# Graph network with two expert layers: what the accumulating stores of the last expert layer wait for

## The reference

```python
rh = jax.nn.relu(features @ router_w1 + router_b1)
expert_logits = jax.nn.softmax(rh @ router_w2 + router_b2, axis=-1)
top_w, top_i = jax.lax.top_k(expert_logits, TOP_K)               # TOP_K = 2
routing_weights = jax.nn.softmax(top_w, axis=-1)
h1 = jax.nn.relu(jnp.einsum('bsd,edh->bseh', features, expert_w1) + expert_b1)
h2 = jax.nn.relu(jnp.einsum('bseh,ehf->bsef', h1, expert_w2) + expert_b2)
expert_out = jnp.einsum('bsef,efo->bseo', h2, expert_w3) + expert_b3
sel = jnp.take_along_axis(expert_out, top_i[:, :, :, None], axis=2)
combined = jnp.sum(sel * routing_weights[..., None], axis=2)
...
x = x + _L1_ffn_ref(_layernorm(x, axis=-1)[None], ...)[0]
```

## Time and profile before

| | before |
|---|---|
| median of 3 runs | 6241.84 us (6240.61 to 6241.86) |
| the profiled execution | 6241.7 us |
| its span | 6240.0 us |
| first matmul group `c` of the expert loop | 5856.15 us |
| first accumulating store, tile 0 | 5860.63 us |
| first store of tile 9 | 5922.40 us |
| first store of tile 53, the last | 6229.75 us |
| PE busy, 5860 to 5940 | 80.00 of 80.00 us |
| DMA to landing, accumulating stores | 2.7 / 3.9 / 5.6 us (min, median, max) |

### The profile page before, as it was taken

The page is one execution under the profiler, slowest core; times in us unless marked ns, Lnnn a source line. Parts: engine busy times, 40 slices in busy tenths (PEclk is TensorE's granted clock), DMA queues, the critical chain, the costliest instruction groups (busy, mean ns, idle before and its releaser), DMA issues.

```text
span 6240.0 us, 87374 instructions
## 1 busy us (share of the span) xinstructions
PE 5227.2 (84%) x24825; PEld 4399.8 (71%) x24825; DVE 3345.8 (54%) x9909; ACT 1339.5 (21%) x3057; POOL 3935.4 (63%) x4345
## 2 busy tenths in 40 slices
PE   0265767489999999989999899899999999987786
PEld 0154555267777777777888788678887888876675
DVE  9867566445555555455445543564454644537422
ACT  0011111011111111124223322241112411112343
POOL 5777777765555555588888885406765067745444
PEclk9977888699999999999999999999999999999898
DMA  1022122233333333711001100213333134365443
GB/s 43 24 78 81 56 60 58 84 105 98 98 100 99 98 99 100 77 43 46 17 17 31 46 17 19 84 49 102 105 99 98 49 102 117 110 96 144 101 76 53
DMA packets 323172, 465.00 MB, mean 75 GB/s; under 512 B 98998, under 2 KB 253050, under 8 KB 322866
## 3 DMA queue, kind: packets, MB, share of 16 engines
q0 software_dynamic: 163312, 261.71, 18.5%
q1 hardware_dynamic: 159554, 199.67, 10.6%
HBM read 359.22 MB, written 102.61 MB: 74 GB/s over the span
## 4 chain that ended last, share of the span: by engine, by line
PE 65%; DMA 12%; POOL 8%; DVE 8%; issue 4%; ACT 1%; DVEq 0%; SPq 0%; POOLq 0%; ACTq 0%
PE bank L2342 19%; PE bank L2353 14%; DMA scratch_sorted<-sb_FREE 7%; POOL scratch_sorted L1020 6%; PE bank L2388 6%; PE bank L2403 6%; PE bank L2570 6%; PE bank L2552 5%; PE bank L2695 3%; PE bank L2333 2%; DMA sb_rows<-scratch_xn,sb_row_of 2%; DMA out<-sb_work_KT,sb_srec 1%; DMA out<-sb_work_TM,sb_srec 1%; DVE sb_STATE L1495 1%; POOL out L1090 1%
## 5 line engine op out<-in xcount | busy, mean ns | idle before, releaser
L1027 POOL DMA_INDIRECT sb_rows<-scratch_xn,sb_row_of x1760 | 1717.7, 976 | 1435.2 <-PE bank L2388 605.8
L1020 POOL DMA_INDIRECT scratch_sorted<-sb_FREE x1564 | 1608.1, 1028 | 486.0 <-issue 334.9
L2353 PE MATMUL bank<-sb_work_FT,sb_W 128*128 128x250 f32 x4400 | 1010.6, 381 | 20.1 <-ACT sb_work_FT L1099 15.5
L1099 ACT ACTIVATE sb_HT<-bank,sb_cols 128x250 f32<-128x250 f32 x1333 | 553.7, 467 | 1987.3 <-PE bank L2552 1061.8
L2353 PEld LDWEIGHTS bank<-sb_work_FT,sb_W 128*128 128x128 f32 x4400 | 847.7, 194 | 135.9 <-ACT sb_work_FT L1099 23.2
L2342 PE MATMUL bank<-sb_W,sb_HT 128*125 128x256 f32 x4000 | 890.8, 379 | 0.7 <-ACT sb_HT L1099 0.7
L2342 PEld LDWEIGHTS bank<-sb_W,sb_HT 128*125 128x125 f32 x4000 | 750.4, 188 | 114.1 <-ACT sb_HT L1099 1.1
L2403 PE MATMUL bank<-sb_rows,sb_work_TM 128*125 128x257 f32 x1760 | 473.3, 393 | 70.5 <-DMA sb_rows<-scratch_xn,sb_row_of 67.7
L1764 DVE TENSOR_TENSOR sb_FREE<-sb_FREE,bank 125x257 f32 x440 | 186.1, 423 | 623.6 <-PE bank L2388 588.4
L1819 DVE TENSOR_TENSOR sb_STATE<-sb_STATE,bank 125x257 f32 x440 | 185.7, 422 | 620.8 <-PE bank L2403 590.1
L2388 PE MATMUL bank<-sb_rows,sb_work_TM 128*125 128x257 f32 x1760 | 441.1, 390 | 38.4 <-DMA sb_rows<-scratch_xn,sb_row_of 29.1
(11 more groups left out here) (382 smaller groups left out, 7034.2 us busy)
## 6 DMA issues: line engine op xcount, KB each, us to landing
sb_rows<-scratch_xn,sb_row_of POOLq DMA_INDIRECT x1760, 2.8
scratch_sorted<-sb_FREE POOLq DMA_INDIRECT x1564, 2.3
scratch_qT<-sb_work_QF SPq DMA_DIRECT2D x100, 250.0 KB
sb_work_QF<-scratch_qT SPq DMA_DIRECT2D x100, 250.0 KB
sb_HT<-scratch_zs SPq DMA_DIRECT2D x54, 261.0 KB, 3.1
sb_work_XC<-in_x SPq DMA_DIRECT2D x50, 250.0 KB
sb_work_ZT<-scratch_xn SPq DMA_DIRECT2D x50, 250.0 KB
sb_W<-in_L_mix_W SPq DMA_DIRECT2D x9, 1024.0 KB
```

The lines of the kernel that those rows point to most:

```text
L1020: nc.gpsimd.indirect_dma_start(out=sorted_d[e], out_offset=bass.IndirectOffsetOnAxis(ap=pos[e][0:n, c:c + 1], axis=0), in_=rec[e][0:n, 2 * ...
L1027: nc.gpsimd.indirect_dma_start(out=rows[:, t % RING, 0:D], out_offset=None, in_=table, in_offset=bass.IndirectOffsetOnAxis(ap=row_of[:, t: ...
L1099: return nc.scalar.activation(dst, source, func, **k)
L2353: ins = nc.tensor.matmul(dst[:, b, :], w[:, k0 + k, 128 * (b0 + b):128 * (b0 + b) + 128], source[:, k, :], start=(n == 0), stop=(n == 2 * ...
```

## The change

POOL's wait ahead of a tile's stores is for other tiles than before. A real tile waits for all tiles of the experts ahead of its own; a padding tile for all tiles ahead of it. How many these are is known only on the chip, so DVE makes a table of counts and POOL reads it.

- The one semaphore `result_added` becomes four, one for each slot of the ring of four; a slot's semaphore goes up by 32 with each of its tiles. DVE's waits for tiles t - 4 and t - 8 and SP's last wait name the slot's semaphore.
- The routing steps get one more, `began_at`, a copy of START.
- `results_due` on DVE, between the preparation of tile 0 and that of tile 1, makes the table `due_of` in ten dependent steps: for a padding tile `began_at` becomes the tile's own number, and then, for each slot q, the number of tiles ahead of `began_at` that used slot q, at least 1, times 32, as integers.
- On POOL, tiles 0 to 3 wait as before. From tile 4 on, four value loads read the tile's counts, after the waits for `at` and `y`, and four waits against these registers, each with a `hold`, stand in place of the one wait against a constant.

The diff, without the new names of tensors and semaphores:

```diff
@@ on SP, at the end @@
-            sp.wait_ge(result_added, 32 * NX)
+            for t in range(NX - XRING, NX):
+                wait(sp, added(t))
@@ names @@
-        result_added = sem("result_added")
+        result_added = [sem(f"result_added_{q}") for q in range(XRING)]
+
+        def added(t):
+            return result_added[t % XRING], 32 * (t // XRING + 1)
@@ on POOL @@
+            pool.wait_ge(order_step, XRING + 6)
             for t in range(NX):
                 q = t % XRING
                 wait(pool, x_dve.done("at", t))
                 wait(pool, x_act.done("y", t))
-                if t:
-                    pool.wait_ge(result_added, 32 * t)
-                hold(pool)
+                if t < XRING:
+                    if t:
+                        wait(pool, added(t - 1))
+                    hold(pool)
+                else:
+                    before = [pool.value_load(due_of[0:1, slot, t:t + 1], min_val=32, max_val=32 * (NX // XRING + 1))
+                              for slot in range(XRING)]
+                    for slot in range(XRING):
+                        pool.wait_ge(result_added[slot], before[slot])
+                        hold(pool)
                 for u in range(2):
                     nc.gpsimd.indirect_dma_start(
...
-                        compute_op=ALU.add).then_inc(result_added, 16)
+                        compute_op=ALU.add).then_inc(result_added[q], 16)
@@ on DVE @@
+            step("began_at", nc.vector.tensor_copy(began_at, START))
             step("exp_all", nc.vector.tensor_copy(exp_all, EXPERTS))
...
+            def results_due():
+
+                def due_step(n, ins):
+                    ins.then_inc(order_step, 1)
+                    dve.wait_ge(order_step, n)
+
+                late = due[:, 0, :]
+                due_step(1, nc.vector.tensor_tensor(late, turn_no, began_at, ALU.subtract))
+                due_step(2, nc.vector.scalar_tensor_tensor(late, real, 0.5, late, ALU.is_lt, ALU.mult))
+                due_step(3, nc.vector.tensor_tensor(began_at, began_at, late, ALU.add))
+                for q in range(XRING):
+                    due_step(4 + q, nc.vector.tensor_scalar(
+                        due[:, q, :], began_at, 1.0 / XRING, (XRING - 1 - q) / XRING - (XRING - 1) / (2.0 * XRING),
+                        ALU.mult, ALU.add))
+                due_step(XRING + 4, nc.vector.tensor_scalar(due, due, ROUND, ROUND, ALU.add, ALU.subtract))
+                due_step(XRING + 5, nc.vector.tensor_scalar(due, due, 1.0, 32.0, ALU.max, ALU.mult))
+                due_step(XRING + 6, nc.vector.tensor_copy(due_of, due))
...
             for b in range(-2, NX + 1):
                 t = b + 2
+                if t == 1:
+                    results_due()
...
-                        dve.wait_ge(result_added, 32 * (t - SRING + 1))
+                        wait(dve, added(t - SRING))
...
-                        dve.wait_ge(result_added, 32 * (t - XRING + 1))
+                        wait(dve, added(t - XRING))
```

More of the change, by code:

```diff
@@ L511, in build @@
         exp_all = carve(NX)
+        began_at = carve(NX, 1)
+        due = carve(XRING * NX, 1).rearrange("p (q t) -> p q t", q=XRING)
+        due_of = carve(XRING * NX, 1).bitcast(I32).rearrange("p (q t) -> p q t", q=XRING)
         SHARES = carve(4 * SRING).rearrange("p (q u k) -> p q u k", q=SRING, u=2)
@@ L575, in build @@
         tile_loaded = [sem(f"tile_loaded_{q}") for q in range(XRING)]
-        result_added = sem("result_added")
+        result_added = [sem(f"result_added_{q}") for q in range(XRING)]
+        def added(t):
+            return result_added[t % XRING], 32 * (t // XRING + 1)
         pads_stored, pads_ready = sem("pads_stored"), sem("pads_ready")
         route_step, route_sums = sem("route_step"), sem("route_sums")
-        out_stored, routing_cleared = sem("out_stored"), sem("routing_cleared")
+        out_stored, routing_cleared, order_step = sem("out_stored"), sem("routing_cleared"), sem("order_step")
         ROUTE_STEPS = ["tiles", "whole", "began", "ended", "done", "row", "real", "in", "rel", "in0",
-                       "last", "exp_of", "in_of", "exp_all"]
+                       "last", "exp_of", "in_of", "began_at", "exp_all"]
         def route(step):
```

## The result

| | before | after |
|---|---|---|
| median of 4 runs | 6241.85 us (6240.61 to 6242.10) | 6177.66 us (6176.16 to 6178.67) |
| ratio | | 0.9898, 95% interval 0.9886 to 0.9911 |
| the profiled execution, its span | 6241.7, 6240.0 us | 6176.16, 6174.4 us |
| first store of tile 0 | 5860.63 us | 5861.12 us |
| first store of tile 50 | 6210.81 us | 6144.74 us |

The kernel is 64 us faster, 1.0%. Forecast were 6176 us, in a range of 6168 to 6205.

What follows compares the result with a forecast made beforehand. POOL's wait for landing, 6.99 us a tile, bounds the later expert phase. Tile 50's store at 6144.4, plus 18.94, 0.5 and 10.25, gives a span of 6174.1; with 1.7 around it, 6176 us, range 6168 to 6205.

Steps and rivals of the forecast that it cites:

- The bound before: Expert phase, later part: POOL sets the pace, descriptors plus waiting for the second store's landing, 6.99 us a tile.
- the ring: Four result tiles absorb POOL's lag of about 1.3 us a tile, until DVE's bias addition waits and holds PE back.
- PE late next: After the change POOL needs 3.70 us a tile, so PE sets the pace: 54 tiles at 5.62 us.
- Which tiles wait: A wait for the predecessor stays at tiles 1 to 4, 24, 26, 47, 48, 51, 52, 53: 11 of 53.
- rival 3: The counts fail and each tile still waits for its predecessor: 6.99 us and more a tile, 6255 us; chance 0.01.
- A boundary: A tile beginning an expert still waits, costing POOL 1.4 us (6.99 against 5.62), caught up at 1.7 a tile.
- v: One whole value load on POOL with register steps: taken as 0.60 us, 2.4 us a tile for four.
- The latency: Loads and waits behind the tile's own result delay its store by 2.8 us (2.4 plus 0.4), without slowing the pace.
- rival 1: POOL's loads don't run beside descriptors: 4.6 + 4v us a tile, runs of 6238 to over 6300 us; chance 0.12.
- The sequencer's own path: POOL's sequencer needs 3.9 us a tile for loads, waits and stores, under 5.62, with descriptor work beside it.
- DVE's table: Ten small DVE steps between preparing tiles 0 and 1, about 2.6 us; tile 1's weights still come 1.5 us early.
- The sum: Tile 50's store at 6144.4, then 18.94 and 0.5 to the last tile, 10.25 to the end: span 6174.1 us.

Runs made afterwards that it cites:

- g2: Kernel after with half of stage c left out, four of its eight matmuls a tile: median 6127.18 us, loop 287.0 us.
- constants: Kernel after with the same four waits against constants for this routing, no value loads and no DVE table: median 6168.11 us, loop 327.5 us.
- loads ahead: Kernel after with POOL's four value loads moved ahead of the waits for row numbers and result: median 6174.59 us, loop 327.8 us.
- g4: Kernel after with value loads ahead of the waits and padding tiles storing nowhere: median 6167.84 us, loop 323.4 us.

## Why the prediction was right

**The bound before.** 6.99 us a tile through landing was the cycle, and the ring the way in which it reached PE. Shown twice: where the wait is kept from tile 26 on, those tiles cost 7.05 us, and half of stage c left out of the kernel before gains nothing.

**PE late next, at 5.62.** The term that carries the sum held to the second decimal, over 48 tiles. g2 shows PE as the bound by taking work from it.

**Which tiles wait.** 24 and 26 show as said; tile 51 starts 7.05 us after 50, and tile 52 5.70 us after the short tile 51. The counts do what they say (rival 3). A boundary cost POOL 2.0 to 2.1 us more than PE's pace, not 1.4: the steps there were 7.64 and 7.75, because the second store of the tile ahead took 4.97 and 4.96 us to land (at tile 24: 1.85 to that store, 4.97 to its landing, 0.81 to the next descriptors, 7.63). In the second profile of the kernel after it is 4.78 and 4.64; with constants 3.65 and 3.67, and the step to tile 24 is 6.32. Why it lands later in the kernel after is not shown. It was hidden anyway.

**The loads.** v was put at 0.60, with 0.57 and 0.74 as ends. Most loads take 0.55, just under the lower end, but the mean is 0.62, since some take longer, and the mean is what adds up. The latency was put at 2.4 for the loads and 0.4 for three more waits. The loads cost 2.65; a wait with its hold is 0.06 in the chain, so three are 0.2, where the 0.16 of the earlier trace rows had been read as the price of one. The two errors cancel: 2.8 us in all, as forecast. That they run beside the descriptors, on which rival 1 hung with 0.12, was inferred from DVE; the trace of after shows it on POOL itself.

**The sequencer's own path.** It was forecast at 3.9 us with four loads, 2.4 for the loads and 1.5 for the rest. The trace of after has 2.49 for the loads, and the runs with eight and twelve loads have 1.5 and 1.4 for the rest, so the forecast stands. Its terms give 4.8 + 1.5 = 6.3 us for eight loads, and 6.32 was measured; the 5.6 to 5.9 that were expected of that run came from the later and smaller v of 0.55. With 1.4 and 0.60, about seven loads a tile would reach PE's 5.62, an estimate.

**DVE's table.** 2.4 us against 2.6, covered as said; loads ahead with the table and constants without it have the same loop.

**The sum.** Tile 50 was forecast at 6144.4 and starts at 6144.74; tiles 51 to 53 were given 19.4 and take 19.36; the rest was 10.25 and is 10.30. The span was forecast at 6174.1 and is 6174.4. One side forecast was wrong: that PE would be full to about 6155. Its last groups began at 6146.04 and ended at 6149.66, since the last tiles have fewer stages beside them. In the kernel after this is hidden by the landings of tiles 50 to 53; in g4, where it is not, it was worth 2.8 us.

## What to carry to other kernels

When an engine that issues DMAs waits for the landing of each before the next, the cost of a turn is descriptors plus landing, and a ring hides it only until it is full; look at whether the other engines' idle time begins after as many turns as the ring's slack allows. A count that only the chip knows can be waited for through a register: put its loads ahead of the wait for data, so that they cost nothing, and add up the sequencer's path from the mean time of a load and not from the usual one, because that path, not the engine's busy time, sets how many loads are free. Test a claimed bound by taking work away from it in both kernels: here the same cut was worth 0 and 44 us.

## What the runs showed of the hardware

- A value load on POOL's sequencer takes 0.55 us in the middle and 0.62 in the mean (0.29 for the TENSOR_LOAD itself in the middle, at most 0.70 among 200) and runs while that engine's own DMA descriptors are being made. By the Trainium skill (DMA: Bandwidth & Descriptors, latency and other measured facts) a tensor load has a floor of about 600 ns. For the instruction alone the measured 0.29 decides; only with its two register steps does a load come near that figure.
- POOL's sequencer is held 0.53 us by each indirect DMA and 0.06 by each wait with its hold: 1.36 us for two DMAs, four register waits and the wait ahead of the next tile's loads (6014.41 to 6015.77, twelve loads a tile).
- Accumulating stores of different rows from two tiles, in flight together every 3.7 us, land as fast as one tile's alone: 4.0 us, over the 56 of 108 stores whose landing the trace gives, against 3.9 at the median, at a DMA share of 0.74 to 0.77.
- Stores whose rows all lie outside the output still cost POOL 1.55 + 0.30 us each in descriptors (6139.51 to 6143.21 for two).
